# A language-model tower in fp32: the experts' biases by one bf16 matmul over 48 rows of part products instead of an fp32 one over 8 rows

## The chip, the cores and the metric

The kernel runs on one core of one Trainium2 chip. The metric is the time of one execution on the device in microseconds, the median of several executions. The profile is of one more execution, and its times are those of that execution alone. The engines are called as in the profile: PE is TensorE (PEld its weight loads), DVE VectorE, ACT ScalarE, POOL GpSimd, SP SyncE.

## The reference

Four sequences of 512 tokens, width 256, one layer: an embedding lookup, a local attention (16 heads of 16, windows of 128), and then a full attention and a mixture of eight experts side by side. The part around the change, cut to its core:

```python
h = h + local_attention(layernorm(h))
x = layernorm(h)
gate = softmax(x @ W_gate + b_gate)                        # 8 experts
top_g, top_i = top_k(gate, 2)
combine = sum(one_hot(top_i, 8) * top_g[..., None], axis=2)   # [B, S, 8], two entries per row are not zero
expert_out = einsum('bsd,edf->bsef', x, W_experts) + b_experts
moe_out = einsum('bsef,bse->bsf', expert_out, combine)
out = h + full_attention(x) + moe_out
```

The change touches one term of it: `combine @ b_experts`, a product of [512, 8] with [8, 256] for each of the four batches.

## The kernel before, in words

The program is written out by hand, each engine with its own list and semaphores between them. The work is cut into eight stages (`STAGES`), each the attention of one kind (LOCAL or FULL) for one batch, in the order local 0, local 1, local 2, full 0, local 3, full 1, full 2, full 3, numbered 0 to 7. A stage has 16 units, a unit two half-slots. In a unit TensorE computes transposed scores (L1493 full, L1499 local, into ST), row scores for the maxima of the heads to come (L1471, L1476 and L1479, into SC), and probabilities times V of an earlier unit (L1520, into OB). VectorE takes the maxima (L980, L985, L988), ScalarE the exponentials (L845, L848), GpSimd masks the local ones (L716).

All other work ("jobs") is put beside it by half-slots. `PREPS` says for each stage which preparation runs there and from which half-slot it counts its steps; the tables of steps (`GATE_STEP`, `COMB_STEP`, `EB_STEP` and others) say at which step each job comes. Jobs use the two PSUM banks R in turn, in one global order (`JOBS`), and TensorE's `claim` waits until the job two places before has been read out. Jobs named below: "shift" turns the maxima of four heads (L1410), which ScalarE copies (L825) and SyncE writes into QS (L512); the scores of those heads wait for that. "o" turns an attention output (L1417), which VectorE normalises (L1018, L1022). Every engine works through its list strictly in order.

The experts' biases go like this for a batch `b`, in the preparation "full" of the batch:

1. VectorE computes the gate's weights in small steps and ends with `comb[b % 2]`, [128, 4 tiles, 8] (L1064), at step 19.
2. TensorE turns it, four fp32 transposes into one bank (`turn_comb`, L1323), at step 22. ScalarE copies the [8, 512] to `combT` (L871).
3. TensorE multiplies, `expert_bias` (L1330), at steps 25 and 27: two tiles each, `combT` of a tile as weights and `exp_bias` [8, 256] as moving data, all fp32.
4. VectorE adds the bank to `h` (`add_biases`, L1119).

Step 22 falls into the last half-slot of stage 1 for batch 0, of stage 3 for batch 1 and of stage 5 for batch 3, and into stage 4 for batch 2. The bias matmuls then fall into the units after it, those of batches 0, 1 and 3 at the start of the stages 2, 4 and 6.

GpSimd's list in a local stage: the mask of unit `u`, then its part of the preparations (the third bf16 part of queries and keys, L702; `add_bo`, L709; `inv_std`, L696 and L698), then in the stages after a full one the addition of the attention (L726). Masked probabilities are multiplied two units later. In the late stages it also issues the gathers of the experts' weights. SyncE's list holds the transfers of parts to the scratch in DRAM (L491), from there into QS and KS (L505), of shift rows (L512), and of sorted rows and their outputs (L559, L565, `x_sorted`, `y_sorted`); `keep_outputs` on VectorE (L1128) waits for the store of `ys` two before.

`xs` are three buffers [128, 2, 256] which are first used in stage 5, for sorted rows.

## Time and profile before

| | us |
|---|---|
| median of 3 runs | 625.78 |
| lowest and highest | 624.35, 626.04 |
| the profiled execution, its own time | 623.86 |
| its span in the trace | 622.1 |
| mean granted clock of TensorE, of full speed | 0.977 |
| span of stage 0 (first scores to first scores of stage 1) | 66 to 110.9 |

The time of the profiled execution is its span and 1.8 us around it. In the page "busy" counts matmuls whose ends overlap, so that the distance between two starts on TensorE is less than the duration shown. A group of rows "x4" in a timeline is four instructions in one row. An idle time in brackets stands before the row and names what ended it.

### The profile page before, as it was taken

The numbers are of one execution on the slowest core, as the hardware profiler recorded it, in microseconds if no ns is written. First come the engines' busy times: TensorE is split into PE (matmuls) and PEld (weight loads), VectorE is DVE, ScalarE is ACT, GpSimd is POOL, SyncE is SP. The second block draws the span as 40 slices with busy tenths as digits, with TensorE's granted clock in tenths as the row PEclk, the third lists the DMA queues.
The fourth block names the chain that finished last, engine by engine and source line by source line (L and its number), as shares of the span: only waits on it lengthen the run. The fifth ranks groups of instructions, "written<-read, shape, count | busy, mean of one in ns | idle before, by whom it ended". The sixth has DMA issues, their size and how long they took to land.

```text
span 622.1 us, 10004 instructions
## 1 busy us (share of the span) xinstructions
PE 559.4 (90%) x3473; PEld 303.9 (49%) x3473; DVE 422.8 (68%) x941; ACT 295.8 (48%) x558; POOL 182.0 (29%) x237
## 2 busy tenths in 40 slices
PE   3887899889999898999898899989999899999996
PEld 2455555655565333434543465544535555554452
DVE  6835757476877888577668776756876665677842
ACT  0321545444644575477354353534555445444444
POOL 6553436222432501022223132401133332033201
PEclk9988999899999999999897799999999999999999
DMA  6477526341353235533415116413158788213311
GB/s 190 103 158 172 126 70 179 53 95 53 110 103 69 86 103 137 136 88 100 86 44 170 50 55 153 115 30 79 59 157 208 211 239 234 71 38 121 114 52 34
DMA packets 42946, 69.23 MB, mean 111 GB/s; under 512 B 7177, under 2 KB 36497, under 8 KB 39825
## 3 DMA queue, kind: packets, MB, share of 16 engines
q1 hardware_dynamic: 38656, 56.01, 35.4%
q0 software_dynamic: 4224, 12.59, 6.9%
q8 instruction: 28, 0.46, 0.3%
q14 instruction: 22, 0.17, 0.1%
q10 hardware_dynamic: 16, 0.01, 0.0%
HBM read 45.25 MB, written 23.07 MB: 110 GB/s over the span
## 4 chain that ended last, share of the span: by engine, by line
PE 64%; DVE 15%; DMA 8%; issue 7%; ACT 3%; SPq 2%; POOL 1%; DVEq 0%; ACTq 0%
PE OB L1520 12%; PE R L1402 9%; PE R L1300 8%; PE SC L1471 7%; PE ST L1493 6%; DVE neg_max L980 5%; PE R L1315 4%; PE SC L1476 3%; PE R L1388 3%; DMA y_sorted<-ys 3%; PE ST L1499 2%; DMA scratch<-parts 2%; PE R L1417 2%; PE R L1348 2%; PE SC L1479 2%
## 5 line engine op out<-in xcount | busy, mean ns | idle before, releaser
L980 DVE TENSOR_REDUCE neg_max<-SC 128x1 f32<-128x512 f32 x256 | 170.9, 686 | 85.2 <-PE SC L1471 81.6
L845 ACT ACTIVATE prob<-ST 128x512 f32<-128x512 f32 x256 | 136.8, 599 | 127.0 <-PE ST L1493 120.1
L1520 PE MATMUL OB<-prob,VS 128*32 128x512 f32 (+2 forms) x1024 | 107.4, 492 | 0.1
L1471 PE MATMUL SC<-KS,QS 96*128 96x512 bf16 x256 | 97.9, 391 | 9.1 <-DVE neg_max L980 7.1
L848 ACT ACTIVATE prob<-ST 128x512 f32<-128x512 f32 (+1 forms) x128 | 68.1, 543 | 74.3 <-PE ST L1499 73.6
L716 POOL TENSOR_SCALAR_AFFINE_SELECT prob<-prob 128x512 f32<-128x512 f32 x64 | 41.0, 641 | 143.2 <-ACT prob L848 143.1
L1493 PE MATMUL ST<-QS,KS 98*128 98x512 bf16 x256 | 78.1, 382 | 2.0 <-ACT prob L845 1.9
L988 DVE TENSOR_REDUCE neg_max<-SC 128x2 f32<-128x512 f32 x64 | 44.0, 688 | 24.3 <-PE SC L1479 24.0
L985 DVE TENSOR_REDUCE neg_max<-SC 128x1 f32<-128x128 f32 (+1 forms) x128 | 39.5, 350 | 28.4 <-PE SC L1479 28.3
L1476 PE MATMUL SC<-KS,QS 96*128 96x256 bf16 (+1 forms) x256 | 54.8, 268 | 3.6 <-DVE neg_max L985 2.1
L1479 PE MATMUL SC<-mask_q,ident_bf 128*128 128x128 bf16 x256 | 51.3, 225 | 0.0
L702 POOL TENSOR_TENSOR parts<-rest,parts 128x512 bf16<-128x512 f32 x32 | 37.3, 1168 | 46.5 <-ACT parts L791 29.9
L1471 PEld LDWEIGHTS SC<-KS,QS 96*128 96x128 bf16 x256 | 25.0, 98 | 51.7 <-DVE neg_max L980 34.3
L1499 PE MATMUL ST<-QS,KS 98*128 98x256 bf16 (+1 forms) x256 | 46.8, 265 | 3.0 <-DMA QS<-shiftT 3.0
L786 ACT ACTIVATE parts<-R,qk_bias 128x512 bf16<-128x512 f32 x32 | 22.0, 687 | 55.1 <-PE R L1300 47.0
L1493 PEld LDWEIGHTS ST<-QS,KS 98*128 98x128 bf16 x256 | 24.7, 98 | 32.0 <-ACT prob L845 11.2
L726 POOL TENSOR_TENSOR h<-h,AO 128x256 f32<-128x256 f32 x15 | 10.8, 725 | 99.1 <-DVE AO L1022 71.5
L953 DVE SCALAR_TENSOR_TENSOR rest<-R,qk_bias,parts 128x512 f32<-128x512 f32 x32 | 23.9, 748 | 21.1 <-ACT parts L786 15.1
L1520 PEld LDWEIGHTS OB<-prob,VS 128*32 128x32 f32 x1024 | 20.4, 109 | 36.0 <-issue 33.1
L1476 PEld LDWEIGHTS SC<-KS,QS 96*128 96x128 bf16 x256 | 25.2, 100 | 26.2 <-issue 9.6
L1300 PE MATMUL R<-xT_full,w_qkv 128*128 128x512 f32 x64 | 33.0, 608 | 3.0 <-DVE VS L965 3.0
L1142 DVE SCALAR_TENSOR_TENSOR h<-R,comb,h 128x256 f32<-128x256 f32 x64 | 27.8, 475 | 8.8 <-PE R L1402 8.8
(148 smaller groups left out, 810.1 us busy)
## 6 DMA issues: line engine op xcount, KB each, us to landing
scratch<-parts SPq DMA_DIRECT2D x96, 128.0 KB
QS<-scratch SPq DMA_DIRECT2D x16, 384.0 KB, 5.2
KS<-scratch SPq DMA_DIRECT2D x16, 384.0 KB, 4.4
QS<-scratch SPq DMA_DIRECT2D x16, 256.0 KB, 3.6
KS<-scratch SPq DMA_DIRECT2D x16, 256.0 KB, 4.3
x_sorted<-ys SPq DMA_DIRECT2D x24, 128.0 KB, 3.2
xs<-x_sorted SPq DMA_DIRECT2D x12, 256.0 KB
y_sorted<-ys SPq DMA_DIRECT2D x12, 256.0 KB, 6.8
```

Of the source, the lines that this page charges most:

```text
L845: act.activation(prob[:, u % 2, e, :], src[:, :], ACT.Exp, scale=SCALE).then_inc(s_prob, 1)
L848: act.activation(prob_local[:, u % 2, u // 2 % 2, 2 * e:2 * e + 2, 0:w], src[:, :].rearrange("p (i w) -> p i w", i=2)[:, :, 0:w], ACT.Exp, ...
L980: dve.tensor_reduce(own_max[:, i, head:head + 1], bank[:, :], AX.X, ALU.max, negate=True).then_inc(s_max, 1)
L988: dve.tensor_reduce(own_max[:, 2:4, head], bank[:, :].rearrange("p (w k) -> p w k", w=2), AX.X, ALU.max, negate=True).then_inc(s_max, 1)
L1300: mm = pe.matmul(bank[:, :], w, xT_of(p)[:, c, :], start=(c == 0), stop=(c == NC - 1))
L1402: mm = pe.matmul(bank[:, t % 2 * D:(t % 2 + 1) * D], xT_full[b % 2][:, c, t * P:(t + 1) * P], w_exp[n % W_RING][:, c, :], start=(c == 0), ...
L1471: pe.matmul(bank[:, :], Q[0:SHIFT_ROW, head, i * P:(i + 1) * P], K[0:SHIFT_ROW, head, :], start=True, stop=True).then_inc(s_sc_ps, 1)
L1476: pe.matmul(bank[:, first:last], Q[0:SHIFT_ROW, head, w * P:(w + 1) * P], K[0:SHIFT_ROW, head, max(w - 1, 0) * P:(w + 1) * P], start=(w % ...
L1479: mm = pe.matmul(bank[:, last - P:last], ident_bf[:, :], mask_q[:, :], start=False, stop=(w % 2 == 1), skip_group_check=True)
L1493: mm = pe.matmul(bank[:, :], K[0:KROWS, g * GH + e, keys], Q[0:KROWS, g * GH + e, :], start=True, stop=True)
L1499: mm = pe.matmul(bank[:, i * 2 * P:i * 2 * P + w], K[0:KROWS, head, keys], Q[0:KROWS, head, kt * P:kt * P + w], start=(i == 0), stop=(i == 1),
L1520: mm = pe.matmul(OB[VW * i:VW * (i + 1), columns], VS[s % 3][:, kt, v:v + VW], p_of, start=(kt == 0), stop=(kt == NT - 1), skip_group_chec ...
```

## The change

The fp32 product is replaced by one over parts. Each fp32 number is written as a sum of three bf16 parts; of the nine products of parts the six with the largest (`BIAS_PRODUCTS`: 0·0, 0·1, 0·2, 1·0, 1·1, 2·0) are put one below the other, so that a matmul over 6 x 8 = 48 rows sums them.

- GpSimd splits the weights of each batch (`split_comb`, new step 20 of the preparation "full"): a cast to the first part, written three times; a subtraction that leaves the rest; a cast of the rest to the second part, written twice; a subtraction for the third part. Each waits for the one before. It waits for VectorE's `comb`, and for TensorE's turn of the batch before.
- TensorE's turn waits for these four steps (`s_comb_parts`) instead of for `comb`. It turns [128, 48] in bf16, and ScalarE copies 48 rows of bf16 instead of 8 of fp32.
- TensorE's bias matmuls are bf16 over 48 rows, two per block as before.
- GpSimd splits the biases once (`split_biases`, stage 0, unit 12): four steps over [8, 256], in buffers of `xs`, into which the biases are loaded now.
- SyncE puts the parts one below the other in `bias_stack` by six transfers of [8, 256] bf16 (`stack_biases`, stage 1, unit 0). TensorE waits for them before the first bias matmul.

The diff without the declarations of three semaphores:

```diff
--- before.py
+++ after.py
@@ -75,6 +75,9 @@
 Q_STEPS = {"first": (9, 10, 11, 12), "later": (9, 11, 13, 15)}
 V_STEPS = {"first": (13, 14), LOCAL: (10, 12), FULL: (8, 8, 9, 10)}
 GATE_STEP, COMB_STEP, EB_STEP = 10, 22, (25, 27)
+SPLIT_STEP = 20
+
+BIAS_PRODUCTS = ((0, 0), (0, 1), (0, 2), (1, 0), (1, 1), (2, 0))
 AO_STEP, WO_STEP = (2, 6), (8, 9)
 GATE_STEPS, DENSE_GATE_STEPS = 16, 12
 READ_LATER = ("q", "ex", "dx", "o", "eb", "route")
@@ -282,13 +285,16 @@
         w_qkv = sb("w_qkv", [P, NC, 3 * D + E])
         w_exp = [w_q, w_k, w_v] + [sb(f"w_exp{k}", [P, NC, D]) for k in range(W_RING - 3)]
         xs = [sb(f"xs{k}", [P, 2, D]) for k in range(X_RING)]
+
+        exp_bias, bias_rest = (xs[k][0:E, 0, :] for k in (1, 2))
+        bias_parts = xs[0][0:E, :, :].bitcast(BF16).rearrange("e j n -> e (j n)")[:, 0:PARTS * D]\
+            .rearrange("e (a n) -> e a n", a=PARTS)
         xsT = [sb(f"xsT{k}", [P, 2 * NC * P]) for k in (0, 1)]
         ys = [sb(f"ys{k}", [P, 2, D]) for k in range(Y_RING)]
         qk_bias = [sb(f"qk_bias{k}", [P, 2, NC]) for k in (0, 1)]
         v_bias = [sb(f"v_bias{k}", [P, D]) for k in (0, 1)]
         o_bias = sb("o_bias", [P, D])
         gate_bias = sb("gate_bias", [P, E])
-        exp_bias = sb("exp_bias", [E, D])
         parts = sb("parts", [P, 4, PARTS, T], BF16)
         rest = sb("rest", [P, 2, T])
         QS = [sb(f"QS{k}", [P, H, T], BF16) for k in (0, 1)]
@@ -325,7 +331,10 @@
         grec = sb("grec", [P, NT])
         above = sb("above", [P, NT, E, E])
         equal = sb("equal", [P, NT, E, E])
-        combT = sb("combT", [E, T])
+        comb_parts = sb("comb_parts", [P, NT, len(BIAS_PRODUCTS), E], BF16)
+        comb_rest = sb("comb_rest", [P, NT, E])
+        combT = sb("combT", [len(BIAS_PRODUCTS) * E, T], BF16)
+        bias_stack = sb("bias_stack", [len(BIAS_PRODUCTS) * E, D], BF16)
         before = sb("before", [P, E, E])
         rank = sb("rank", [P, NT, E])
         chosen = sb("chosen", [P, NT, E])
@@ -482,7 +494,7 @@
             sp.dma_start(v_bias[FULL][:, :], bqkv[2 * D:3 * D].rearrange("(a n) -> a n", a=1).to_broadcast([P, D]))\
                 .then_inc(s_w2, 16)
             sp.dma_start(gate_bias[:, :], bg.rearrange("(a n) -> a n", a=1).to_broadcast([P, E])).then_inc(s_w2, 16)
-            sp.dma_start(exp_bias[:, :], bexp).then_inc(s_w2, 16)
+            sp.dma_start(exp_bias, bexp).then_inc(s_w2, 16)
 
             def write_parts(p, m):
                 for i in (2 * m, 2 * m + 1):
@@ -545,6 +557,11 @@
                     for e in range(E):
                         if step == DENSE_W_STEP + 4 * e:
                             load_weights(b, e)
+
+            def stack_biases():
+                sp.wait_ge(s_bias_parts, 4)
+                for n, (_, a) in enumerate(BIAS_PRODUCTS):
+                    sp.dma_start(bias_stack[n * E:(n + 1) * E, :], bias_parts[:, a, :]).then_inc(s_bias_stack, 16)
 
             def zero_sorted(j):
 
@@ -595,6 +612,8 @@
                     for t in (2 * u, 2 * u + 1):
                         for what, c, first in PREPS[s]:
                             prep(what, c, t - first)
+                    if (s, u) == (1, 0):
+                        stack_biases()
                     if s == 3 and u == 0:
                         sp.wait_ge(s_iota, 3)
                     if s == 3 and u < EXPERT_TILES // 2:
@@ -716,6 +735,37 @@
                 pool.affine_select(out=own, in_=own, compare_op=ALU.is_ge, fill=0.0, base=0,
                                    pattern=[[0, GH], [1, P]], channel_multiplier=-1).then_inc(s_masked, 1)
 
+            def split_biases():
+                pool.wait_ge(s_w2, 16 * OTHER_LOADS)
+                pool.tensor_copy(bias_parts[:, 0, :], exp_bias).then_inc(s_bias_parts, 1)
+                pool.wait_ge(s_bias_parts, 1)
+                pool.tensor_tensor(bias_rest, exp_bias, bias_parts[:, 0, :], ALU.subtract)\
+                    .then_inc(s_bias_parts, 1)
+                pool.wait_ge(s_bias_parts, 2)
+                pool.tensor_copy(bias_parts[:, 1, :], bias_rest).then_inc(s_bias_parts, 1)
+                pool.wait_ge(s_bias_parts, 3)
+                pool.tensor_tensor(bias_parts[:, 2, :], bias_rest, bias_parts[:, 1, :], ALU.subtract)\
+                    .then_inc(s_bias_parts, 1)
+
+            def split_comb(b):
+
+                n = at(b, 4, 0)
+                pool.wait_ge(s_comb, b + 1)
+                if b > 0:
+                    pool.wait_ge(s_comb_ps, b)
+                rows = comb[b % 2][:, :, :]
+                pool.tensor_copy(comb_parts[:, :, 0:3, :], rows.unsqueeze(2).to_broadcast([P, NT, 3, E]))\
+                    .then_inc(s_comb_parts, 1)
+                pool.wait_ge(s_comb_parts, n + 1)
+                pool.tensor_tensor(comb_rest[:, :, :], rows, comb_parts[:, :, 0, :], ALU.subtract)\
+                    .then_inc(s_comb_parts, 1)
+                pool.wait_ge(s_comb_parts, n + 2)
+                pool.tensor_copy(comb_parts[:, :, 3:5, :], comb_rest[:, :, :].unsqueeze(2).to_broadcast([P, NT, 2, E]))\
+                    .then_inc(s_comb_parts, 1)
+                pool.wait_ge(s_comb_parts, n + 3)
+                pool.tensor_tensor(comb_parts[:, :, 5, :], comb_rest[:, :, :], comb_parts[:, :, 3, :], ALU.subtract)\
+                    .then_inc(s_comb_parts, 1)
+
             def add_attention(b, g):
                 pool.wait_ge(s_norm, G * STAGE[FULL, b] + g + 1)
                 pool.wait_ge(s_yb, at(b, 2, 2))
@@ -735,6 +785,8 @@
                             third_part(p, i)
                     if what == "local" and step == q_step(p)[3] + 4:
                         add_bo(b)
+                    if what == "full" and step == SPLIT_STEP:
+                        split_comb(b)
                 if what == "route":
                     for n in range(PAIR_TILES * TOP_K):
                         if step == SCATTER_STEP + n:
@@ -766,6 +818,8 @@
                         mask(s, u)
                     if (s, u) == (0, 4):
                         gather(3)
+                    if (s, u) == (0, 12):
+                        split_biases()
                     for t in (2 * u, 2 * u + 1):
                         if s >= STAGE[LOCAL, B - 1]:
                             pool.wait_ge(s_st_ps, begun(s, t))
@@ -868,7 +922,8 @@
                         act.wait_ge(s_comb_ps, b + 1)
                         if b > 0:
                             act.wait_ge(s_eb_ps, at(b, 2, 0))
-                        act.copy(combT[:, :], bank_of(("comb", b, 0))[0:E, :]).then_inc(s_combT, 1)
+                        turned = bank_of(("comb", b, 0))[:, :].bitcast(BF16)
+                        act.copy(combT[:, :], turned[0:len(BIAS_PRODUCTS) * E, 0:T]).then_inc(s_combT, 1)
                 if what == "out":
                     for c in range(NC):
                         if step == AO_STEP[c]:
@@ -1317,17 +1372,20 @@
                 mm.then_inc(s_v_ps, 1)
 
             def turn_comb(b):
-                bank = claim(("comb", b, 0))
-                pe.wait_ge(s_comb, b + 1)
+                turned = claim(("comb", b, 0))[:, :].bitcast(BF16)
+                pe.wait_ge(s_comb_parts, at(b, 4, 4))
                 for t in range(NT):
-                    mm = pe.transpose(bank[0:E, t * P:(t + 1) * P], comb[b % 2][:, t, :], ident[:, :])
+                    mm = pe.transpose(turned[0:len(BIAS_PRODUCTS) * E, t * P:(t + 1) * P],
+                                      comb_parts[:, t, :, :].rearrange("p n e -> p (n e)"), ident_bf[:, :])
                 mm.then_inc(s_comb_ps, 1)
 
             def expert_bias(b, j):
                 bank = claim(("eb", b, j))
                 pe.wait_ge(s_combT, b + 1)
+                if b == 0:
+                    pe.wait_ge(s_bias_stack, 16 * len(BIAS_PRODUCTS))
                 for t in (2 * j, 2 * j + 1):
-                    mm = pe.matmul(bank[:, (t % 2) * D:(t % 2 + 1) * D], combT[:, t * P:(t + 1) * P], exp_bias[:, :],
+                    mm = pe.matmul(bank[:, (t % 2) * D:(t % 2 + 1) * D], combT[:, t * P:(t + 1) * P], bias_stack[:, :],
                                    start=True, stop=True)
                 mm.then_inc(s_eb_ps, 1)
 ```

GpSimd's list at the end of stage 0's preparations, before the change. The rows are the additions of `add_bo` in unit 10, the masks up to unit 1 of stage 1 and on, and the `inv_std` of the next preparation:

```order
L716 AFFINE_SELECT prob<-prob 128x4x128
L709 TENSOR_TENSOR h<-h,o_bias 128x256 x4
L716 AFFINE_SELECT prob<-prob 128x4x128 x11
L696 TENSOR_TENSOR var_eps<-var,eps 128x4
L698 TENSOR_TENSOR rstd<-var_eps,minus_half 128x4
```

The same place of the list with the change:

```order
L735 AFFINE_SELECT prob<-prob 128x4x128
L728 TENSOR_TENSOR h<-h,o_bias 128x256 x4
L735 AFFINE_SELECT prob<-prob 128x4x128 x2
L740 CAST xs<-xs 8x256
L742 TENSOR_TENSOR xs<-xs 8x256
L745 CAST xs<-xs 8x256
L747 TENSOR_TENSOR xs<-xs 8x256
L735 AFFINE_SELECT prob<-prob 128x4x128 x9
```

The four steps of the biases stand between the masks of units 12 and 13.

GpSimd's list at the end of stage 1, where batch 0's weights are split, before the change:

```order
L702 TENSOR_TENSOR parts<-rest,parts 128x512
L716 AFFINE_SELECT prob<-prob 128x4x128
L702 TENSOR_TENSOR parts<-rest,parts 128x512
L716 AFFINE_SELECT prob<-prob 128x4x128 x8
L696 TENSOR_TENSOR var_eps<-var,eps 128x4
```

And with it:

```order
L721 TENSOR_TENSOR parts<-rest,parts 128x512
L735 AFFINE_SELECT prob<-prob 128x4x128
L757 CAST comb_parts<-comb 128x4x24
L760 TENSOR_TENSOR comb_rest<-comb,comb_parts 128x32
L763 CAST comb_parts<-comb_rest 128x4x16
L766 TENSOR_TENSOR comb_parts<-comb_rest,comb_parts 128x4x8
L735 AFFINE_SELECT prob<-prob 128x4x128 x7
```

Of the eight masks that stood in one row the first, of unit 14, is ahead of the split now, and that of unit 15 behind it.

SyncE's list around the start of stage 1 with the change. The first row are the shift rows of stage 1's first four heads, the third those of the next four; before, both stood in one row of four:

```order
L524 DMA QS<-shiftT 1x4x512 x2
L564 DMA bias_stack<-xs 8x256 x6
L524 DMA QS<-shiftT 1x4x512 x2
L517 DMA QS<-scratch 48x1x4096
L517 DMA KS<-scratch 48x4096
```

The six small transfers stand between the two pairs of shift rows.

## Rows read from the trace of the kernel before

**Rows 1.** Page, part 1: engine, busy us, share of the span, instructions
```profile
PE 559.4 (90%) x3473; PEld 303.9 (49%) x3473; DVE 422.8 (68%) x941; ACT 295.8 (48%) x558; POOL 182.0 (29%) x237
```

**Rows 2.** Groups by line and shape, TensorE (busy us, mean ns | idle before)
```profile
L1330 PE MATMUL R<-exp_bias,combT 8*128 8x256 f32 x32 | 9.0, 400 | 3.0 <-DVE AO L1022 3.0
```

**Rows 3.** Timeline of TensorE: start us, us, engine line op out<-in xcount [idle before]
```profile
110.87 0.39 PE L1499 MATMUL ST<-QS,KS 98*128 98x256 bf16 x2 [2.34 <-DMA QS<-shiftT]
...
162.51 0.60 PE L1323 MATMUL R<-ident,comb 128*8 128x128 f32 x4
...
285.48 0.39 PE L1410 MATMUL R<-ident_bf,shift 128*8 128x128 bf16 x4
285.80 0.28 PE L1476 MATMUL SC<-KS,QS 96*128 96x256 bf16 x1
285.92 0.22 PE L1479 MATMUL SC<-mask_q,ident_bf 128*128 128x128 bf16 x1
...
288.59 0.60 PE L1323 MATMUL R<-ident,comb 128*8 128x128 f32 x4
289.03 0.27 PE L1476 MATMUL SC<-KS,QS 96*128 96x256 bf16 x1
...
291.85 1.13 PE L1330 MATMUL R<-exp_bias,combT 8*128 8x256 f32 x4
292.91 0.23 PE L1476 MATMUL SC<-KS,QS 96*128 96x128 bf16 x1
...
297.44 1.13 PE L1330 MATMUL R<-exp_bias,combT 8*128 8x256 f32 x4 [0.83 <-DVE AO L1022]
...
348.28 0.39 PE L1410 MATMUL R<-ident_bf,shift 128*8 128x128 bf16 x4 [0.97 <-DVE h L1119]
...
463.79 1.13 PE L1330 MATMUL R<-exp_bias,combT 8*128 8x256 f32 x4 [1.30 <-DVE AO L1022]
```

**Rows 4.** Timeline of VectorE
```profile
94.30 0.93 DVE L997 CAST shift<-neg_max 128x16 bf16<-128x16 f32 x1
...
103.24 0.17 DVE L999 TENSOR_TENSOR shift<-neg_max,shift 128x16 bf16<-128x16 f32 x1
...
161.44 0.19 DVE L1064 TENSOR_TENSOR comb<-chosen,grec 128x32 f32<-128x32 f32 x1
...
167.80 0.62 DVE L985 TENSOR_REDUCE neg_max<-SC 128x1 f32<-128x128 f32 x2 [0.99 <-PE SC L1479]
...
285.56 0.19 DVE L1064 TENSOR_TENSOR comb<-chosen,grec 128x32 f32<-128x32 f32 x1
...
291.73 0.69 DVE L988 TENSOR_REDUCE neg_max<-SC 128x2 f32<-128x512 f32 x1 [0.88 <-PE SC L1479]
...
296.96 0.42 DVE L1022 TENSOR_TENSOR AO<-R,rden 128x256 f32<-128x256 f32 x1
...
343.32 0.69 DVE L980 TENSOR_REDUCE neg_max<-SC 128x1 f32<-128x512 f32 x1 [0.53 <-PE SC L1471]
```

**Rows 5.** Groups by line and shape, GpSimd
```profile
L702 POOL TENSOR_TENSOR parts<-rest,parts 128x512 bf16<-128x512 f32 x32 | 37.3, 1168 | 46.5 <-ACT parts L791 29.9 <-PE ST L1493 16.6
...
L726 POOL TENSOR_TENSOR h<-h,AO 128x256 f32<-128x256 f32 x15 | 10.8, 725 | 99.1 <-DVE AO L1022 71.5 <-DVE h L1142 26.4 <-PE ST L1493 0.7
...
L698 POOL TENSOR_TENSOR rstd<-var_eps,minus_half 128x4 f32<-128x4 f32 x8 | 8.3, 1034 | 0.6
...
L650 POOL CAST tile_no<-tile_int 128x24 f32<-128x24 int32 x1 | 0.2, 216 | 0.0
```

**Rows 6.** Timeline of GpSimd, stage 0
```profile
101.99 0.63 POOL L716 TENSOR_SCALAR_AFFINE_SELECT prob<-prob 128x512 f32<-128x512 f32 x1 [0.62 <-ACT prob L848]
```

**Rows 7.** Timeline of ScalarE, stage 0
```profile
104.60 0.56 ACT L825 COPY shiftT<-R 8x512 bf16<-8x512 bf16 x1
```

**Rows 8.** Waits: engine line waited for: us in total, times, longest us
```profile
DVE ys L1128 <- DMA y_sorted<-ys: 4.8, 4, 1.9
```

**Rows 9.** One stretch of the span: busy by engine, PEclk, DMA share, GB/s
```profile
112.00:116.00 4.00, 4.00 (x31) 3.54 (x26) 1.87 (x6) 2.70 (x5) 0.83 (x2) 0.57 0.01 4
```

3 lines of the change are left out of this document (added).

## The prediction, made before the change was run

> **What bounds the kernel now.** First the busy shares [rows 1]: TensorE is busy for 559.4 of the 622.1 us, VectorE for 422.8, GpSimd for only 182.0. So most microseconds taken from TensorE's queue should come off the end, and most that GpSimd gets more are free, unless somebody waits for them. Then the group of the bias matmuls [rows 2]: 32 records for 16 matmuls, because an fp32 matmul runs as two passes. They come in eight blocks of two matmuls, two blocks for each batch. Their busy sum of 9.0 us isn't what they cost, since records overlap; the price is the distance from one start to the next start on TensorE, read in its timeline [rows 3]. Last, for each block, what TensorE or VectorE waits for just behind it [rows 3, 4]: that decides whether the saved time reaches the end.
>
> **The bias matmuls.** The block at 291.85 is followed by the next matmul at 292.91: 1.06 us [rows 3]. Afterwards it is two bf16 matmuls of 256 columns over 48 rows. The nearest row is a bf16 matmul of 256 columns over 96 rows, from 285.80 to the next start at 285.92: 0.12 us, of which I take 0.11, as two of them follow each other. The new block costs 0.22 us and saves 0.84. Eight blocks make 6.7 us on TensorE's own queue.
>
> **The turning of the weights.** Four fp32 transposes take from 288.59 to 289.03, 0.44 us; four bf16 ones of the same number of moving columns from 285.48 to 285.80, 0.32 us [rows 3]. That is 0.12 us per batch. The full saving on the queue is then 6.7 + 0.5 = 7.2 us.
>
> **What of it reaches the end**, batch by batch.
> Batch 0 (end of stage 1, start of stage 2). Behind the first block VectorE waits for a row of scores, 0.99 us before 167.80 [rows 4], so it can follow a TensorE that is 0.84 us earlier. Behind the second nobody is late. All passes: 1.68 us.
> Batch 1 (stages 3 and 4). VectorE starts at 291.73 and has no gap until it ends the normalisation at 296.96 + 0.42 = 297.38 (no row between carries an idle time); TensorE waits for exactly that before the second block at 297.44 [rows 3, 4]. VectorE's string of work starts before the first block does, so that block's 0.84 us only lengthens TensorE's wait. The second block's 0.84 and the turn's 0.12 pass: 0.96 us.
> Batch 2 (stage 4, beside a full stage's maxima). VectorE had waited 0.53 us before 343.32 [rows 4] and then has no gap until after TensorE has waited for it at 348.28 [rows 3]. It can move up by that 0.53 us and no further; of 2 x 0.84 us the rest turns into a longer wait. 0.53 us.
> Batch 3 (stages 5 and 6). TensorE waits 1.30 us for VectorE before the second block at 463.79 [rows 3], but there VectorE itself waits for the rows of scores before it, and moves up with them. 1.68 + 0.12 = 1.80 us.
> Together 1.68 + 0.96 + 0.53 + 1.80 = 4.97 us.
>
> **GpSimd's four steps for a batch's weights, and who waits.** TensorE's turn now waits for GpSimd, which waits for VectorE's weights. In batch 0 VectorE ends them at 161.44 + 0.19 = 161.63 and TensorE wants them at 162.51 [rows 3, 4]: 0.88 us. The four steps are a cast of 96 columns, a subtraction of 32, a cast of 64, a subtraction of 32, each waiting for the one before. GpSimd's subtraction of 512 columns takes 1168 ns, its addition of 256 columns 725 ns, a cast of 24 columns 216 ns [rows 5]; by the slope of the first two, 1.73 ns a column, 32 columns take 0.34 us, and the casts 0.22 to 0.34, for which I take 0.28. With five hand-overs of 0.06 us (297.38 to 297.44) that is 2 x 0.34 + 2 x 0.28 + 0.3 = 1.54 us. TensorE waits 1.54 - 0.88 = 0.66 us, less the 0.12 of the faster turn: 0.54 us lost. Bounds: 0.1 us if a step takes only the 216 ns of the small cast (1.16 us in all), and 3.6 us if each takes the 1034 ns that a power of four columns takes. Behind the split on GpSimd stands the mask of unit 15; its user comes two units later, and it hides. In batch 1 there is room from 285.75 to 288.59, 2.84 us [rows 3, 4]; batches 2 and 3 leave more. There the split costs nothing; without that cover it would cost 1.5 us each time.
>
> **GpSimd's four steps for the biases.** They start behind the mask that ends at 101.99 + 0.63 = 102.62 [rows 6]. Two subtractions of 256 columns at 0.73 us, two casts between 0.22 and 0.73, taken as 0.45, and three hand-overs: 2.5 us, to about 105.2. The next mask comes 1.5 us late and is used after 106.8, so it hides. What may not hide is VectorE's cast and subtraction of the shift around 103.0 to 103.4. Beside a GpSimd subtraction this cast took 0.93 us [rows 4]; the subtraction at 103.24 stood alone and took 0.17. The shift goes by TensorE and ScalarE to the transfer for which TensorE waits 2.34 us at 110.87 [rows 3]: each microsecond of delay there is a microsecond of the end. ScalarE takes up the turned shift only at 104.60 [rows 7], some 0.27 us after TensorE has it, which covers a short delay. I take 0.1 us; bounds 0 and 0.9.
> The Trainium skill, "SBUF — State Buffer", section "SBUF: two separate sides", speaks against this place: the port that VectorE and GpSimd share is held for a whole instruction and the other blocks. By it one of the two short VectorE steps waits for the end of a whole GpSimd subtraction and the term would be 0.5 us, not 0.1.
>
> **The six small transfers** stand on SyncE's queue behind the shift rows of stage 1, which are on their way before them, and ahead of nothing that is due before unit 2. The same queue's other work at that time waits for TensorE anyway. I cost them at 0, bounds 0 and 0.3 us, if they slow the landing before 110.87. ScalarE's copy of 48 rows for 8 has as many columns: 0.
>
> **Tail.** Between 470 and 530 VectorE waits four times, 4.8 us in all, for stores of sorted outputs [rows 8]. Transfers that run at their own pace can eat part of batch 3's gain: I take 0.3 us, bounds 0 and 1.8.
>
> **Sum.** 4.97 - 0.54 (batch 0's stall, net) - 0.1 - 0.3 = 4.0 us. The profiled execution took 623.86 us (span 622.1), so 619.9 for it; the median of the runs is 625.78, 1.9 above the profiled one, and 4.0 below it is **621.8 us**.
>
> **The rivals.**
> *All of it passes.* TensorE's queue bounds throughout and VectorE's strings of work in batches 1 and 2 turn out elastic: 625.8 - 7.2 = 618.6, or 619.2 with the stall. For it: 90% busy. Against it: the waits at 297.44 and 348.28 [rows 3].
> *Absorbed.* VectorE's fixed strings, the stores of stage 6 and the clock take nearly everything. The clock: behind the 2.34 us wait TensorE's granted clock is 0.57 on average from 112 to 116 [rows 9], so about 3.4 us at 1.2 GHz instead of 2.4, which cost 1.7 us. The change makes waits longer: before 296.2 and 348.3 by 0.84 us each, and a new one at 162.5. One more such stretch leaves 2.3 us of 4.0, two leave 0.6: about 625. The Trainium skill, "TensorE: Matmul & The Clock Gate", section "What's actually happening", ties the clock to how busy the array has been; by it the blocks that shrink while TensorE waits anyway could have just this price. Against it: the 1.30 us wait at 463.79 was followed by no fall of the clock.
> *GpSimd is slow (slower than before).* If each of its small steps costs what the power does, 1.03 us, a split takes 4.4 us. Batch 0 then stalls 3.5 us and batch 1 4.4 - 2.84 = 1.6, less the 0.12; the biases' split of 4.3 us holds the shift back by 0.9; and two stalls of that size each bring a clock stretch of 1.7: 4.97 - 3.5 - 1.6 - 0.9 - 3.4 - 0.3 = -4.7, about 630.5. It decides from steps of about 0.8 us on: stalls of 2.5, 0.7 and 0.9 us and one stretch of the slow clock then outweigh 4.97 - 0.3. Against it: the cast of 24 columns at 216 ns.
> *The change doesn't do what it says*: if 48-row matmuls ran at the old pace, there would be only the stall, 626.5. The bf16 rows at 285.80 speak against it.
>
> **Numbers.** 0.3% (1.9 us) is about what a measurement of this kernel can tell from no change. Forecast (620.5 to 623.3) 0.50; all passes 0.17; absorbed 0.22; GpSimd slow 0.07; not as said 0.04. Faster by over 0.3% are the first two and a little of the third: 0.70. Within 0.3%: 0.22. Slower: 0.08. The range reaches from 618.5 (all passes) to 625.9 (absorbed with both the costs unknown at their bounds).
>
> **What would show it.** Start to start of a bias block 0.2 to 0.25 us, of a turn 0.32. A TensorE wait for GpSimd of about 0.65 us before the first turn, none before the other three. VectorE's waits for scores shorter behind batches 0 and 3; TensorE's waits for VectorE before the batch 1 and batch 2 marks longer by about 0.8 us. The bias split on GpSimd about 2.5 us long, and TensorE's wait at the start of stage 1 still near 2.3 us. Wrong, if GpSimd's small steps take 0.5 us or more, if the number of stretches at 1.2 GHz changes, or if stage 6 swallows batch 3's gain.

## The result, and the profile after

| | before | changed |
|---|---|---|
| median of 20 executions each, us | 624.69 (620.13 to 626.77) | 618.01 (615.18 to 622.59) |
| ratio, 95% interval | | 0.9922 (0.9901 to 0.9944) |
| profiled execution, us | 623.86 | 618.68 |
| its span, us | 622.1 | 616.9 |
| its mean granted clock | 0.977 | 0.978 |

The ratio is a gain of 4.9 us (3.5 to 6.2). A ratio leaves out the few executions, five of the 231 used below, that ran over 1.5% above the fastest of their kernel. The forecast was a gain of 4.0 and 621.8 us, with a range from 618.5 to 625.9. The plain median, 618.01, lies 0.5 us below that range, but the kernel before ran faster in this comparison too (624.69) than the 625.78 that the forecast started from; the ratio on 625.78 gives 620.9, inside the range. Against the kernel before on the same chip, the measured gain is a little above the forecast. Two more measurements of the unchanged new kernel stand below.

First the page of the changed kernel, part 1, which answers to [rows 1]:
```profile
PE 553.9 (90%) x3457; PEld 298.5 (48%) x3457; DVE 422.1 (68%) x941; ACT 296.1 (48%) x558; POOL 188.8 (31%) x257
```
TensorE has 16 records fewer (each of the 16 fp32 matmuls had two) and is busy 5.5 us less. GpSimd has 20 records more and is busy 6.8 us more. VectorE and ScalarE stand as before.

Then the groups by line and shape of the changed kernel, TensorE's first and GpSimd's behind them (busy us, mean ns | idle before). The first answers to [rows 2]:
```profile
L1388 PE MATMUL R<-bias_stack,combT 48*128 48x256 bf16 x16 | 3.1, 274 | 3.0 <-DVE AO L1077 3.0
...
L1378 PE MATMUL R<-ident_bf,comb_parts 128*48 128x128 bf16 x16 | 1.6, 222 | 0.5 <-POOL comb_parts L766 0.5
```
The idle time before the bias matmuls is 3.0 us in both kernels: the same three blocks, the second ones of batches 0, 1 and 3, wait for the same normalisation (L1077, which was L1022). The second row shows the only time that TensorE waits for GpSimd's parts: 0.5 us, once.

TensorE's timeline in the changed kernel (start us, us, engine line op, out<-in, xcount [idle before]). Each row with a number in brackets in the text answers to a row of [rows 3]:
```profile
110.43 0.39 PE L1557 MATMUL ST<-QS,KS 98*128 98x256 bf16 x2 [2.51 <-DMA QS<-shiftT]
...
162.66 0.38 PE L1378 MATMUL R<-ident_bf,comb_parts 128*48 128x128 bf16 x4 [0.48 <-POOL comb_parts L766]
162.97 0.28 PE L1534 MATMUL SC<-KS,QS 96*128 96x256 bf16 x1
...
287.15 0.40 PE L1378 MATMUL R<-ident_bf,comb_parts 128*48 128x128 bf16 x4
287.49 0.28 PE L1534 MATMUL SC<-KS,QS 96*128 96x256 bf16 x1
...
290.31 0.39 PE L1388 MATMUL R<-bias_stack,combT 48*128 48x256 bf16 x2
290.64 0.23 PE L1534 MATMUL SC<-KS,QS 96*128 96x128 bf16 x1
...
294.55 0.39 PE L1468 MATMUL R<-ident_bf,shift 128*8 128x128 bf16 x4 [2.24 <-DVE h L1174]
295.77 0.39 PE L1388 MATMUL R<-bias_stack,combT 48*128 48x256 bf16 x2 [0.83 <-DVE AO L1077]
...
342.48 0.20 PE L1417 MATMUL R<-sel,tri 128*128 128x64 bf16 x1 [0.61 <-DVE h L1174]
...
345.08 0.39 PE L1468 MATMUL R<-ident_bf,shift 128*8 128x128 bf16 x4 [0.97 <-DVE h L1174]
...
459.40 0.39 PE L1388 MATMUL R<-bias_stack,combT 48*128 48x256 bf16 x2 [1.30 <-DVE AO L1077]
459.72 0.39 PE L1529 MATMUL SC<-KS,QS 96*128 96x512 bf16 x1
```
Read two things. The first is the price: a bias block now takes 290.64 - 290.31 = 0.33 us start to start, and 0.32 at 459.40, where it took 1.06. Six of the eight blocks stand like this; the two of batch 2 are followed after 0.42 us (339.25) and 1.00 (341.48, with the wait of 0.61 that stands at 342.48). A turn takes 0.31 and 0.34 us instead of 0.44. The second is how the lead over the kernel before grows, row against row: 0.44 us at the start of stage 1 (110.43 for 110.87); a loss of 0.15 at the turn of batch 0 (162.66 for 162.51); a lead of 1.44 at the turn of batch 1 (287.15 for 288.59), 1.54 at its first block (290.31 for 291.85), 1.67 at its second (295.77 for 297.44), 3.20 at the shift of 345.08 (348.28) and 4.39 at the last row (463.79). TensorE's wait behind batch 1's first block has grown from 1.64 us, in the row that follows from the kernel before, to the 2.24 at 294.55:
```profile
296.22 0.39 PE L1410 MATMUL R<-ident_bf,shift 128*8 128x128 bf16 x4 [1.64 <-DVE h L1119]
```
At 342.48 is a wait of 0.61 us, behind batch 2's second block, in a place where the kernel before had none.

VectorE's timeline in the changed kernel. The rows at 161.03, 167.10 and 295.29 answer to [rows 4], and the last to its row at 343.32, which is now the last of a group of three:
```profile
102.33 0.17 DVE L1052 CAST shift<-neg_max 128x16 bf16<-128x16 f32 x1
102.54 0.52 DVE L1054 TENSOR_TENSOR shift<-neg_max,shift 128x16 bf16<-128x16 f32 x1
...
161.03 0.19 DVE L1119 TENSOR_TENSOR comb<-chosen,grec 128x32 f32<-128x32 f32 x1
...
167.10 0.62 DVE L1040 TENSOR_REDUCE neg_max<-SC 128x1 f32<-128x128 f32 x2 [0.26 <-PE SC L1537]
...
295.29 0.42 DVE L1077 TENSOR_TENSOR AO<-R,rden 128x256 f32<-128x256 f32 x1
...
338.92 1.89 DVE L1035 TENSOR_REDUCE neg_max<-SC 128x1 f32<-128x512 f32 x3 [0.18 <-PE SC L1529]
```
The wait before 167.80 was 0.99 us and is 0.26; the wait of 0.53 before 343.32 is gone. Those are the two places in which VectorE had waited for rows of scores behind a first block.

GpSimd's timeline in the changed kernel: the split of the biases in stage 0, and the split of batch 0's weights in stage 1:
```profile
101.88 0.39 POOL L740 CAST xs<-xs 8x256 bf16<-8x256 f32 x1
102.35 0.68 POOL L742 TENSOR_TENSOR xs<-xs 8x256 f32<-8x256 f32 x1
103.09 0.39 POOL L745 CAST xs<-xs 8x256 bf16<-8x256 f32 x1
103.56 0.66 POOL L747 TENSOR_TENSOR xs<-xs 8x256 bf16<-8x256 f32 x1
...
161.29 0.27 POOL L757 CAST comb_parts<-comb 128x96 bf16<-128x96 f32 x1 [0.35 <-DVE comb L1119]
161.64 0.25 POOL L760 TENSOR_TENSOR comb_rest<-comb,comb_parts 128x32 f32<-128x32 f32 x1
161.95 0.24 POOL L763 CAST comb_parts<-comb_rest 128x64 bf16<-128x64 f32 x1
162.27 0.24 POOL L766 TENSOR_TENSOR comb_parts<-comb_rest,comb_parts 128x32 bf16<-128x32 f32 x1
```
A small step of GpSimd takes 240 to 270 ns and starts 0.31 to 0.35 us behind the one before, so the split of the weights is over 162.66 - 161.22 = 1.44 us after VectorE's weights. Compare 102.54 of VectorE with 102.35 of GpSimd: VectorE's subtraction takes 0.52 us instead of 0.17 [rows 4], and ends where GpSimd's does (103.06 and 103.03). It takes 0.52 or 0.53 us in the two repeats and in split_idle and dve_split too.

### The profile page after: what moved, and what is told of

It reads as the page before. It is cut to its first block, busy times and chain, and to the rows that moved or that the text cites. A ratio compares the mean times of both kernels' runs of the same rounds, so it can differ in the third digit from the quotient of the medians.

```text
span 616.9 us, 10001 instructions
## 1 busy us (share of the span) xinstructions
PE 553.9 (90%) x3457; PEld 298.5 (48%) x3457; DVE 422.1 (68%) x941; ACT 296.1 (48%) x558; POOL 188.8 (31%) x257
## 4 chain that ended last, share of the span: by engine, by line
PE 66%; DVE 16%; DMA 7%; issue 4%; ACT 3%; SPq 2%; POOL 2%; DVEq 0%; ACTq 0%; POOLq 0%
PE OB L1578 12%; PE R L1460 9%; PE SC L1529 8%; PE R L1355 8%; PE ST L1551 6%; DVE neg_max L1035 5%; PE R L1370 4%; PE SC L1534 3%; PE R L1446 3%; PE ST L1557 2%; DMA scratch<-parts 2%; PE R L1475 2%; PE R L1406 2%; DMA y_sorted<-ys 2%; PE SC L1537 2%
## 5 line engine op out<-in xcount | busy, mean ns | idle before, releaser
L1035 DVE TENSOR_REDUCE neg_max<-SC 128x1 f32<-128x512 f32 x256 | 170.7, 686 | 83.2 <-PE SC L1529 82.1
L1529 PE MATMUL SC<-KS,QS 96*128 96x512 bf16 x256 | 97.7, 390 | 8.6 <-DVE neg_max L1035 6.7
L735 POOL TENSOR_SCALAR_AFFINE_SELECT prob<-prob 128x512 f32<-128x512 f32 x64 | 41.1, 643 | 133.3 <-ACT prob L902 133.2
L1534 PE MATMUL SC<-KS,QS 96*128 96x256 bf16 (+1 forms) x256 | 54.7, 268 | 3.1 <-DVE neg_max L1040 1.6
L1040 DVE TENSOR_REDUCE neg_max<-SC 128x1 f32<-128x128 f32 (+1 forms) x128 | 39.5, 350 | 26.1 <-PE SC L1537 25.8
L721 POOL TENSOR_TENSOR parts<-rest,parts 128x512 bf16<-128x512 f32 x32 | 37.4, 1170 | 46.0 <-ACT parts L845 29.4
L1537 PE MATMUL SC<-mask_q,ident_bf 128*128 128x128 bf16 x256 | 51.0, 224 | 0.0
L1557 PE MATMUL ST<-QS,KS 98*128 98x256 bf16 (+1 forms) x256 | 47.1, 266 | 3.0 <-DMA QS<-shiftT 3.0
L1529 PEld LDWEIGHTS SC<-KS,QS 96*128 96x128 bf16 x256 | 24.9, 97 | 51.5 <-DVE neg_max L1035 34.1
L1534 PEld LDWEIGHTS SC<-KS,QS 96*128 96x128 bf16 x256 | 25.2, 100 | 25.9 <-DVE neg_max L1040 9.8
```

Source lines behind the costliest of these rows:

```text
L1035: dve.tensor_reduce(own_max[:, i, head:head + 1], bank[:, :], AX.X, ALU.max, negate=True).then_inc(s_max, 1)
L1529: pe.matmul(bank[:, :], Q[0:SHIFT_ROW, head, i * P:(i + 1) * P], K[0:SHIFT_ROW, head, :], start=True, stop=True).then_inc(s_sc_ps, 1)
L1534: pe.matmul(bank[:, first:last], Q[0:SHIFT_ROW, head, w * P:(w + 1) * P], K[0:SHIFT_ROW, head, max(w - 1, 0) * P:(w + 1) * P], start=(w % ...
L1537: mm = pe.matmul(bank[:, last - P:last], ident_bf[:, :], mask_q[:, :], start=False, stop=(w % 2 == 1), skip_group_check=True)
L1557: mm = pe.matmul(bank[:, i * 2 * P:i * 2 * P + w], K[0:KROWS, head, keys], Q[0:KROWS, head, kt * P:kt * P + w], start=(i == 0), stop=(i == 1),
```

## The experiments

All times are medians; a ratio stands against the kernel before on the same chip in the same comparison, whose medians were 623.11 (first four labels), 621.75 (next four) and 623.59 us (last three).

**One correction, used below.** Executions of one kernel in one comparison lie 4 to 12 us apart here, more than most of the effects. Their times follow the mean granted clock: one straight line through the 231 executions, 91 of them of the kernel before, with a level for each kernel, has a slope of 0.38 us for each 0.001 of the clock, and leaves a scatter of 1.3 us. "At equal clock" means the distance of the levels, with a 95% interval. The changed kernel's 36 executions in three comparisons stand 3.95 +- 0.49 us below the kernel before. That is a statistical correction, not a second measurement: if an edit itself changes the clock, its effect is taken out with it. It has a second weakness. The 20 executions of the kernel before in the first comparison have no clock on record, so the 20 changed ones beside them are set against executions of other comparisons. Without these 20, and with a level for each comparison as well, the changed kernel stands 4.7 +- 0.7 us below the kernel before, and every distance from the changed kernel moves; where that matters, the second number is given as "by comparison".

### The changed kernel again

No edit. It was run twice more, to see which parts of the lead return in other executions.

> The changed kernel again, unchanged, as the base of this group and for the part of the difference that the change can't have made. In the first pair of traces 0.6 of the 5.2 us lay before 47 us, ahead of anything that the change touches, and 0.5 us was a wait for a transfer of expert weights at 378 us. If both are accident (my theory), this run's trace shows the same marks at 165, 172, 299, 343, 459 and 465 us moved by the same steps as the first (+0.6, -1.5, -0.9, -0.6, -0.8, -0.8), while the steps at 47 and 378 us change their size or sign; the ratio to before is 0.993 to 0.994 (4.0 us). If the change of buffers made them (rival), both come again with the same size and the ratio is 0.992.

Measured: 616.17 us, ratio 0.9899 (0.9866 to 0.9932), span 617.0.

> The changed kernel a third time, as the base for the two beside it. Over the runs so far a kernel's time goes with its mean granted clock (slope about -0.36 us per 0.001); at a granted clock of 0.975 the changed kernel stands 3.3 +- 0.6 us and, in the second group, 4.6 +- 1.0 us below the kernel before. Theory: 3.5 to 4.0 us again, ratio 0.994.

Measured: 617.52 us, ratio 0.9918 (0.9891 to 0.9944), span 614.2. The intervals of the three measurements overlap. The spans differ by 2.8 us, and the windows below show one reason; another is that at 100 us the executions already stand up to 2 us ahead of or behind the kernel before, whatever the kernel. One row is the start of stage 1 (108 to 118 us) and one is stage 4 (290 to 300); first the changed kernel, then its second repeat. Columns: busy us (xinstructions) of PE, PEld, DVE, ACT, POOL, then the granted clock, DMA share, GB/s.
```profile
108.00:118.00 10.00, 7.57 (x68) 5.73 (x69) 4.48 (x14) 4.89 (x9) 1.63 (x3) 0.83 0.04 6
290.00:300.00 10.00, 6.93 (x62) 4.01 (x60) 8.39 (x27) 3.94 (x8) 3.37 (x6) 0.83 0.33 84
```
```profile
108.00:118.00 10.00, 8.56 (x94) 6.35 (x95) 6.09 (x17) 6.36 (x13) 2.54 (x4) 1.00 0.11 29
290.00:300.00 10.00, 7.20 (x52) 4.09 (x53) 6.95 (x23) 2.88 (x6) 3.38 (x6) 0.66 0.45 80
```
In the repeat TensorE stays at 2.4 GHz behind the wait at the start of stage 1 (from 110 to 116 us its VectorE work gains 1.7 us on the kernel before, and 0.2 in the changed kernel), and its clock is lower at 290 to 300. The wait there was 2.51 us in the changed kernel, and in the repeat it is:
```profile
109.44 0.39 PE L1557 MATMUL ST<-QS,KS 98*128 98x256 bf16 x2 [1.75 <-DMA QS<-shiftT]
```
What is the same in all three traces are the steps of the lead at the edited places, all but batch 1's; the table of the next section has them.

The expectations were met in part. The step at 47 us changed its size (-0.08 us in the first repeat, for 0.59) and so did the one at 378 (some 1.7 us in both repeats, for 0.1), so both are accident. But batch 1 gave 0.5 us and not 0.9, and the first repeat's ratio was 0.9899, with 0.993 to 0.994 expected: these lie above its interval, and the rival's 0.992 lies inside. The three ratios come to 4.9, 6.3 and 5.1 us, all above the forecast's 4.0.

### Which blocks reach the end: 16 and 7 repeated matmuls

```diff
-                for t in (2 * j, 2 * j + 1):
+                extra = 16 if (b, j) == (1, 0) else 0
+                for t in (2 * j,) * extra + (2 * j, 2 * j + 1):
```
The first matmul of one block is run 16 times more, into the same columns: in batch 1's first block (pad_first, the edit shown) or its second (pad_second, with `(1, 1)`). The later pair has 7 for 16.

> 16 matmuls more (the same product again) in batch 1's FIRST bias block alone, 16 x 0.107 = 1.7 us of TensorE's queue. Theory of the prediction (VectorE's string of work from 291.7 to 297.4 sets the pace there): TensorE's wait behind the block shrinks by 1.7 us and the end moves by 0 to 0.3 us. Rival (TensorE's queue bounds throughout, all 7.2 us were to be had): +1.7 us, ratio to the unpadded kernel 1.0028.

Measured: 618.00 us, ratio 0.9938 (0.9906 to 0.9971), span 616.1.

> The same 16 matmuls in batch 1's SECOND bias block. Theory and rival agree here: nothing waits behind it that would hide it, +1.7 us at the end, and the mark at 299 us moves by +1.7. If it doesn't, both are wrong about what bounds stage 4.

Measured: 620.39 us, ratio 0.9972 (0.9946 to 0.9998), span 618.5. At equal clock the second costs 1.6 +- 0.8 us more than the changed kernel, the first 0.3 +- 0.8 (by comparison 2.5 +- 1.0 and 1.1 +- 1.0). TensorE's timeline with the first block enlarged:
```profile
288.11 2.14 PE L1389 MATMUL R<-bias_stack,combT 48*128 48x256 bf16 x18
290.18 0.23 PE L1535 MATMUL SC<-KS,QS 96*128 96x128 bf16 x1
...
293.49 0.39 PE L1469 MATMUL R<-ident_bf,shift 128*8 128x128 bf16 x4 [1.64 <-DVE h L1174]
```
The block takes 2.07 us instead of 0.32, and the wait behind it is again the 1.64 us of the kernel before: only 0.6 of the 1.75 us went into the wait. By the starts of the same VectorE instructions, 1.0 us reached the work right behind it, so the cover is 0.75 us; the 0.1 us that is left is taken up below, under "Batch 1". In VectorE's timeline it shows as a wait for scores inside the string that had none before or after the change:
```profile
290.67 0.62 DVE L1040 TENSOR_REDUCE neg_max<-SC 128x1 f32<-128x128 f32 x2 [0.90 <-PE SC L1538]
```
The enlarged block is longer than the fp32 one ever was; I had not seen that its 1.7 us exceed the cover. So the test was repeated with 7, which brings the block back to its old length:

> Seven matmuls more (0.75 us, what the change saves per block) in batch 1's FIRST bias block alone. The run with 16 showed that 1.0 of 1.7 us came through: VectorE's string of work covers some 0.7 us. Theory: 0.75 us fits under that cover, so the marks of VectorE behind the block (the maxima at 293.4 us of the kernel before) move by 0 to 0.15 us, and TensorE's wait before the next turn of maxima falls from 2.24 us to about 1.6. Rival (no cover, the queue bounds): +0.75 us there.

Measured: 619.13 us, ratio 0.9937 (0.9904 to 0.9969), span 616.1.

> The same seven in batch 1's SECOND block: the mark at 299 us of the kernel before moves by +0.75 us (theory and rival). With 16 it moved by 3.6 us in a trace in which a stretch at 1.2 GHz lay over them, so this run also tells whether 1.7 or more was the price of the matmuls at full clock.

Measured: 619.07 us, ratio 0.9961 (0.9936 to 0.9986), span 617.4. At equal clock both stand within 0.1 +- 0.9 us of the changed kernel (by comparison 0.9 and 1.1 us above it, +- 1.1): 0.75 us is too little for the end time to tell. The timeline tells it. With 7 in the first block:
```profile
290.98 1.15 PE L1389 MATMUL R<-bias_stack,combT 48*128 48x256 bf16 x9
292.06 0.23 PE L1535 MATMUL SC<-KS,QS 96*128 96x128 bf16 x1
...
295.38 0.39 PE L1469 MATMUL R<-ident_bf,shift 128*8 128x128 bf16 x4 [1.64 <-DVE h L1174]
```
The block is 1.08 us, the old 1.06, and the wait is the old 1.64 instead of 2.24. From 290 to 299 us VectorE's work gains 0.70 us on the kernel before, where it gains 0.83 in the changed kernel: the seven matmuls of 0.75 us cost 0.13. The first block of batch 1 is paid out of a wait. With the same seven in the second block VectorE's work loses 1.10 us there instead of gaining 0.83. In this run, as in pad_second and in the two repeats, the second block ran at 1.2 GHz, so the repeats, which gain 0.39 us from 290 to 299, are the fair comparison: the seven cost 1.49 us, and the 16 of pad_second (3.02 lost) 3.41. Both are 0.213 us for each matmul, which is the distance between their starts in these traces: in the second block they reach what follows in full. The expectation for the seven, 0.75 us, was the price at 2.4 GHz, which neither run shows.

### The stall alone: the splits with nothing gained

```diff
-                    mm = pe.transpose(turned[0:len(BIAS_PRODUCTS) * E, t * P:(t + 1) * P],
-                                      comb_parts[:, t, :, :].rearrange("p n e -> p (n e)"), ident_bf[:, :])
+                    mm = pe.transpose(turned[0:E, t * P:(t + 1) * P], comb[b % 2][:, t, :], ident[:, :])
...
-                    mm = pe.matmul(... combT[:, t * P:(t + 1) * P], bias_stack[:, :],
+                    mm = pe.matmul(... combT[:, t * P:(t + 1) * P], exp_bias,
```
Turn and product are the fp32 ones of before, and the biases have their own buffer again. GpSimd's splits, the six transfers and TensorE's wait for the split stay; their result is not used.

> The fp32 product and fp32 turn of before, with all that GpSimd and SyncE got in the change (both splits, six transfers) and with TensorE's turn waiting for the split, whose result isn't used. Theory: the only price is the wait before batch 0's turn, +0.6 us at the mark at 165 us and nothing at the other batches nor at the start of stage 1: ratio to before 1.001. Rival (the splits, the shared port or the six transfers cost more in places that the faster product hid): +1.5 us or more, with steps at 111 us or in stages 4 and 6.

Measured: 624.59 us, ratio 1.0032 (1.0006 to 1.0059), span 621.4; at equal clock +0.9 +- 0.8 us against before (by comparison 1.2 +- 0.8). In the trace the only slip at an edited place is behind the first turn's wait:
```profile
163.49 0.60 PE L1378 MATMUL R<-ident,comb 128*8 128x128 f32 x4 [0.48 <-POOL comb_parts L767]
```
VectorE's work slips by 0.55 us there, that is by 0.45 as in the changed kernel and by the turn's 0.12. At 103.5 us, beside the split of the biases, it slips by 0.35 us, and has 0.26 of that back by 106.5; behind the six transfers nothing of it is left. At none of the eight blocks does it gain, other than by a stretch of the clock. The other moves of this trace (1.2 us lost at 295 to 299 at 1.2 GHz, 2.2 us won between 356 and 381 us) have no edit near them. So the gain of the changed kernel comes from TensorE's shorter matmuls, and the only price of the splits that the trace shows is the one stall. The ratio itself is a loss of 2.0 us (0.4 to 3.7), more than the theory's 0.6 and no less than the rival's 1.5. The clock explains part of it (a mean of 0.9725, and 0.9743 for the kernel before beside it); whether executions that were not profiled paid more somewhere else, no run shows.

### The split on VectorE

```diff
                    dve.tensor_tensor(comb[b % 2][:, :, :], ...)
...
+                    dve.tensor_copy(comb_parts[:, :, 0:3, :], ...)
...
+                    dve.tensor_tensor(comb_rest[:, :, :], ...)
...
+                    dve.tensor_copy(comb_parts[:, :, 3:5, :], ...)
...
+                    dve.tensor_tensor(comb_parts[:, :, 5, :], ...)
...
-                    if what == "full" and step == SPLIT_STEP:
-                        split_comb(b)
```

> The weights are split by VectorE right behind the weights themselves instead of by GpSimd; the biases still by GpSimd. Four VectorE steps of some 0.18 us and the waits between them are 0.75 to 0.9 us on VectorE per batch. Theory: TensorE's wait before batch 0's turn goes (-0.5 us), but in stage 4 (batch 2), where VectorE is behind, its string grows by 0.8 us, and batch 1 and 3 lie beside idle time of VectorE: -0.5 + 0.8, the end within 0.5 us of the changed kernel. Rival (GpSimd's share is what makes the gain, since VectorE is near the bound everywhere): 2 us slower than the changed kernel or more.

Measured: 618.93 us, ratio 0.9951 (0.9927 to 0.9974), span 615.8; at equal clock 0.1 +- 0.8 us below the changed kernel (by comparison 0.9 +- 1.1 above it). VectorE's timeline, then TensorE's:
```profile
160.05 0.21 DVE L1105 CAST comb_parts<-comb 128x96 bf16<-128x96 f32 x1
160.29 0.19 DVE L1108 TENSOR_TENSOR comb_rest<-comb,comb_parts 128x32 f32<-128x32 f32 x1
160.52 0.20 DVE L1111 CAST comb_parts<-comb_rest 128x64 bf16<-128x64 f32 x1
160.75 0.19 DVE L1114 TENSOR_TENSOR comb_parts<-comb_rest,comb_parts 128x32 bf16<-128x32 f32 x1
```
```profile
161.09 0.38 PE L1373 MATMUL R<-ident_bf,comb_parts 128*48 128x128 bf16 x4
```
The turn's wait is down to 0.13 us, but each batch puts some 0.9 us on VectorE. By the starts of the same VectorE instructions, batch 0 has cost 0.86 us at 167 us (0.45 in the changed kernel), of which 0.34 comes back before 283; batch 3 costs 0.65 us just before 452. In batches 1 and 2 nothing is lost. So the expectation had the wrong place for the price: it put it in stage 4. At the end the two ways cost the same within what can be measured.

### The turn one half-slot later

```diff
-GATE_STEP, COMB_STEP, EB_STEP = 10, 22, (25, 27)
+GATE_STEP, COMB_STEP, EB_STEP = 10, 23, (25, 27)
```

> The turn of the weights one half-slot later (COMB_STEP 23 for 22), with the bias blocks where they were. Theory: the only price of GpSimd's split is TensorE's wait of 0.48 us before batch 0's turn, since GpSimd ends 1.2 us after VectorE and TensorE comes 0.9 us after it; half a slot is over 1.3 us, so the wait goes and the end comes 0.5 us earlier (ratio to the changed kernel 0.999). Rival: the wait is only moved, as TensorE or ScalarE then waits between the turn and the first bias block: 0 or slower.

Measured: 619.43 us, ratio 0.9929 (0.9894 to 0.9963), span 619.7.

> The late turn again. Its trace had no wait before batch 0's turn and the step of +0.6 us at 165 us was gone, yet its median was no better than the changed kernel's, with a mean granted clock of 0.970 for 0.975. Theory: the low clock was accident; at equal clock it is 0.5 to 1 us faster than the changed kernel, and the clock of this group is within 0.002 of the changed kernel's. Rival: the later turn itself brings more stretches at 1.2 GHz (behind the waits of stage 4): clock 0.970 again and no gain in the median.

Measured: 618.21 us, ratio 0.9928 (0.9901 to 0.9955), span 619.3. The stall is gone, as TensorE's timeline shows for the first of the two:
```profile
162.73 0.39 PE L1557 MATMUL ST<-QS,KS 98*128 98x256 bf16 x2
163.05 0.40 PE L1378 MATMUL R<-ident_bf,comb_parts 128*48 128x128 bf16 x4
163.39 0.23 PE L1534 MATMUL SC<-KS,QS 96*128 96x128 bf16 x1
```
VectorE's work slips by 0.02 us across it in both traces, where it slips by 0.45 in the changed kernel. In batch 1 the later turn costs 0.14 us more, in batch 3 it gives 0.20 more, so 0.5 us should be left. At equal clock the 24 executions are 0.8 +- 0.7 us faster than the changed kernel, but by comparison only 0.2 +- 0.8: a gain is not shown. Neither median is lower, and the mean granted clock of both groups is: 0.970 and 0.971, against 0.976 for the changed kernel's 36 executions. That is what the rival of the second expectation forecast, not its theory (within 0.002), and the distance of the two groups together, 0.005 +- 0.003, is more than the scatter of the clocks explains. In the first trace the stretches at 1.2 GHz lay at 49 to 59 us, long before the edited place, and again near 295, 329 and 349 us. The last run tested whether TensorE's waits in stage 4 pull the clock down: the late turn, with 7 repeated matmuls in batch 1's first and batch 2's second block, which would otherwise be waiting.

> The late turn, and seven repeated matmuls (0.75 us) in batch 1's first and batch 2's second bias block, where TensorE's saved time only lengthens its wait for VectorE. Theory on the waits: VectorE's marks at 293.4 and 348 us move by 0 to 0.2 us each, so the fill costs 0 to 0.4 us. On the clock: if the longer waits were what brings the stretches at 1.2 GHz behind them (rival of the prediction), the fill takes back part and the mean granted clock is higher than the late turn's by 0.002 or more (0.7 us); if the stretches come from the waits that were there before the change too, clock and time stay as they are within 0.5 us.

Measured: 617.63 us, ratio 0.9891 (0.9861 to 0.9922), span 620.0. The theory on the waits held: against the first late turn, VectorE's work is held back by 0.16 us behind batch 1's fill and by 0.03 behind batch 2's. On the clock the run decides nothing. Its mean over the 12 executions is 0.9733, and 0.9706 over the 24 of the late turn: 0.0027 higher, which is past the 0.002 that the expectation named for the rival, but with an interval of +- 0.0055. The profiled execution, with a clock of 0.966, has the same stretches at 1.2 GHz in stage 4 as the first trace of the late turn. At equal clock it is 0.5 +- 0.8 us below the changed kernel (by comparison 0.1 +- 0.9), no better than the late turn alone. So the late turn came with a lower clock in two comparisons, by what mechanism stays open, and so does whether the longer waits have to do with it and whether it is a better kernel.

## Why the prediction was right, and where its terms were off

The mechanism was right: where TensorE is late for VectorE a shorter block reaches the end, and where VectorE has an unbroken string it only lengthens TensorE's wait. The lead was followed by the start of the same VectorE instruction in both traces, which are the same 941 in the same order. All columns are set against the one trace of the kernel before, and share its accidents:

| Step (us from, to, in the kernel before) | Predicted, us | Changed kernel | Its two repeats |
|---|---|---|---|
| split of the biases, shift, transfers (100 to 107) | -0.1 | -0.09 | -0.09, -0.09 |
| stall of batch 0, net of the turn (163 to 167) | -0.54 | -0.45 | -0.45, -0.45 |
| batch 0, two blocks (167 to 175) | 1.68 | 1.47 | 1.46, 1.47 |
| batch 1, turn and second block (285 to 299) | 0.96 | 0.93 | 0.48, 0.48 |
| batch 2 (336 to 344) | 0.53 | 0.73 | 0.69, 0.69 |
| batch 3, turn and two blocks (452 to 466) | 1.80 | 1.56 | 1.56, 1.56 |
| tail (466 to the end) | -0.3 | 0.04 | -1.35, -0.06 |

Without the first step, whose 0.09 us ends in the wait at 110.87, the changed kernel's steps come to 4.28 us where the same terms of the prediction come to 4.13; the repeats' come to 2.39 and 3.69. That the sum is nearer than its terms is luck: the blocks of batches 0 and 3 gave 0.45 us less than forecast, and batch 2, the stall and the tail 0.63 more. Its span is 5.2 us shorter. The rest is where nothing was changed: 0.42 us by which this execution was ahead already at 163 us, 0.36 between 356 and 440 us, and 0.09 at 300. The repeats move there by other amounts (2.04 and 3.05 us ahead at 163). The largest such move has a chain of its own. From the issue of stage 1's shift rows to the first scores it took 5.69 us in the kernel before, 5.95 in the changed kernel and 5.28 and 5.19 in the repeats, and the wait in front of those scores changed with it (2.34, 2.51, 1.84 and 1.75 us); behind the two long waits stood 3.4 us at 1.2 GHz, behind the two short ones none.

**A block (0.22 us predicted, 0.32 measured).** This is the term that was most wrong. I took two distances of 0.11 us, from the row at 285.80. The block's second matmul starts 0.12 us behind the first, but what follows starts only 0.20 us behind the second: the blocks at 290.31 and 459.40 are followed by the next start after 0.33 and 0.32. The fp32 block has the same 0.1 us at its end (its last record is followed after 0.31 us, those before it after 0.22), so it could have been read before. It isn't simply the change to another kind of matmul, since that stood behind the row at 285.80 too; what makes it, no run shows. A block saves 0.74 us and not 0.84. The reason given for the 32 records, two passes for each fp32 matmul, says more than the trace does: it shows two records for each, whose starts are 0.22 us apart, twice the distance of bf16 matmuls of as many columns (0.11 in pad_first). The turn was right, at 0.31 to 0.34 us for the 0.32 predicted.

**The stall (0.54).** The split takes 1.44 us from the end of the weights to the turn and not 1.54, as the small steps take 0.25 us and not 0.28 to 0.34. With the room of 0.88 us that the prediction read, the turn starts 0.56 us late for the 0.66 predicted (the view marks 0.48 of it as idle); net of the faster turn 0.45 reach VectorE. The bounds, 0.1 and 3.6, were far wider than the truth, and by their own numbers they are 0.16 and 3.4; the cast of 24 columns was the row to trust, and the power told nothing on the other steps.

**Batch 1.** As predicted to 0.03 us in the changed kernel, in part by luck. The turn gives 0.10 and the second block 0.70. The first block gives nothing through TensorE's queue, as predicted: VectorE's lead stays at 1.54 us through its whole string of work. Then it jumps to 1.67 at one instruction, by a way that the prediction did not have: a subtraction of 4 columns (`apart`, a step of the next layernorm). In the kernel before it takes 0.30 us and ends at 295.02, as GpSimd's mask does (294.37 + 0.63 = 295.00); in the changed kernel the mask is over before it begins, and it takes 0.17. First the kernel before, VectorE and GpSimd, then the changed kernel:
```profile
294.72 0.30 DVE L928 TENSOR_TENSOR apart<-stats 128x4 f32<-128x4 f32 x1
294.37 0.63 POOL L716 TENSOR_SCALAR_AFFINE_SELECT prob<-prob 128x512 f32<-128x512 f32 x1 [2.73 <-ACT prob L848]
```
```profile
293.19 0.17 DVE L983 TENSOR_TENSOR apart<-stats 128x4 f32<-128x4 f32 x1
```
It takes 0.30 or 0.31 us in all five traces in which the first block is long (before, pad_first, pad7_first, late_fill, split_idle) and 0.17 in the other eight, and that is the 0.13 us that pad7_first lost. In the changed kernel's two repeats half of batch 1's gain is missing, since in these the stretch at 1.2 GHz lay over the second block (granted clock 0.66 from 290 to 300 in the second, 0.83 in the changed kernel).

**Batch 2 (0.53).** The cap was the wait, as predicted: 0.61 us came with the 0.53 us wait that went, and the rest of the blocks' saving stands as the new 0.61 us at 342.48. The other 0.12 came in two small steps before it; I had left this batch's turn out of the sum.

**The port.** The page of the Trainium skill that I weighed in the prediction, "SBUF — State Buffer", section "SBUF: two separate sides", was right about the row: VectorE's subtraction took 0.52 us, 0.35 more than alone. It cost nothing at the end all the same. The cast before it had begun 0.02 us ahead of GpSimd's subtraction and took its usual 0.17, and TensorE turned the shift only when its own queue had come to it. Its turn in the changed kernel and in the one before, then ScalarE's copy in the changed kernel:
```profile
103.24 0.39 PE L1468 MATMUL R<-ident_bf,shift 128*8 128x128 bf16 x4
```
```profile
103.94 0.39 PE L1410 MATMUL R<-ident_bf,shift 128*8 128x128 bf16 x4
```
```profile
103.90 0.56 ACT L879 COPY shiftT<-R 8x512 bf16<-8x512 bf16 x1
```
VectorE's cast is 0.70 us ahead of the kernel before (102.33 for 103.03), TensorE's turn is 0.70 ahead and ScalarE's copy too (103.90 for 104.60). So the hold was hidden by TensorE's queue, which came to the shift 0.18 us after the subtraction's end, and the wait of ScalarE that the prediction named was not needed. VectorE's own work was 0.35 us late for a moment, and the 0.09 us of it that it did not win back went into the wait at 110.87. VectorE's share of the price was my 0.1; the shift's share was nothing.

**The transfers and the tail.** The six transfers cost nothing that a run shows: from the issue of the shift rows ahead of them to the first scores of stage 1 it takes 4.8 to 6.3 us in the twelve traces with them, 5.5 on average, and 5.69 in the one without. ScalarE's copy of 48 rows takes 0.58 us for the 0.57 of 8. The 0.3 us of the tail was not lost in the changed kernel, and 1.35 us were in its first repeat: the tail moves from execution to execution by more than the term. As a mean the term can't be called right or wrong.

**The rivals.** *All of it passes* falls by the 0.61 and 2.24 us waits and by pad7_first, though the plain medians, 6.7 us apart, come near its 7.2. *GpSimd is slow* falls by the rows of its steps. *Absorbed* falls, but its mechanism exists: whether a stretch of 1.2 GHz lies over a block decides half of batch 1's gain. As a whole the clock went the other way than this rival feared. In the two comparisons that have the clocks of both kernels the changed kernel's mean is 0.003 +- 0.002 higher, which by the slope is worth 1.1 us, about what the ratios have above the forecast; at equal clock the gain is 3.95 us, or 4.7 by comparison. Whether the change itself raises the clock is not shown. The sign that the prediction named, another number of stretches at 1.2 GHz, came in part: there are seven in the traces of both kernels and six in each repeat, where the one at the start of stage 1 is missing.

## What to carry to other kernels

Price a shorter block on the queue's own clock, from a start to the start of the next kind of instruction *in the place where the block stands*; then ask at each place which engine is late just behind it, and cap the gain there by that engine's wait. Repeating an idle matmul until the block has its old length shows in one trace whether a saving is real, but the padding must not exceed the cover. Before a small gain is put down to a queue, look whether one instruction has become shorter. Where executions scatter by more than the effect, compare the starts of the same instructions of an engine whose program did not change, and set times against the granted clock.

## What the runs showed of the hardware

- The time of this kernel follows TensorE's mean granted clock by 0.38 us for each 0.001, over 231 executions. The places of the stretches at 1.2 GHz differ between executions of one kernel. Behind the wait at the start of stage 1 the clock fell in seven of the 13 traces: behind all six waits of 2.34 us or more (2.34 in the kernel before [rows 3, 9], 2.51 in the changed one), and behind one of 1.64 (pad_first). It did not behind six waits of 1.35 to 2.17 us (1.84 and 1.75 in the two repeats). Others stand near 328 and 348 us in all 13 traces and near 295 in 11, where TensorE waits for VectorE. The two without one near 295 are pad_first and pad7_first, in which the first block is long and the wait behind it 1.64 us; but the kernel before, split_idle and late_fill, with the same wait, have one there, so no rule follows. In pad_second the 18 matmuls took 4.02 us at 1.2 GHz, and the 18 of pad_first 2.14 us at 2.4 GHz:
```profile
295.18 4.02 PE L1389 MATMUL R<-bias_stack,combT 48*128 48x256 bf16 x18 [0.84 <-DVE AO L1077]
```
- Three short VectorE instructions took longer beside GpSimd's work and ended within 0.03 us of GpSimd's instruction: the shift's subtraction 0.52 us for 0.17 beside a subtraction, `apart` 0.30 for 0.17 beside a mask, and the shift's cast 0.93 for 0.17 beside the subtraction of 512 columns that ends at 95.20 [rows 4, 5].
- GpSimd's subtraction of 256 columns on 8 partitions takes 0.66 to 0.68 us, hardly less than the 0.73 of its addition of 256 columns on 128 partitions [rows 5].
- VectorE's steps of the split take 0.19 to 0.21 us, GpSimd's 0.24 to 0.27. For tensors this small the engines differ little, and the hand-overs do: 0.03 to 0.04 us between VectorE's steps in dve_split, 0.06 to 0.08 between GpSimd's.
